# Projections for the next layer in parts of 128 columns, and the denominators of a half in the middle of the next

## The reference

```python
x = x + _L0_xattn_ref(_layernorm(x), ctx_768, Wq, bq, Wk, bk, Wv, bv, Wo, bo)   # 16 heads of 8
...
x = x + _L1_xattn_ref(_layernorm(x), ctx_768, Wq, Wk, Wv, Wo, bo)               # 16 heads of 64
# in _L1_xattn_ref:
k = (context @ Wk).reshape(B, Nk, 16, 64)
v = (context @ Wv).reshape(B, Nk, 16, 64)
```

## Time and profile before

| | |
|---|---|
| three runs, median (lowest, highest) | 3643.95 us (3641.63, 3647.71) |
| profiled execution, span | 3638.8 us |
| first half of layer 0's attention | from 62.14 us to about 161.96 us |
| second half | 161.96 to 260.66 us |
| third half | 260.66 to 359.19 us |
| last half ends | about 852 us |

### The profile page before, as it was taken

How to read it: one execution, slowest core, us unless ns; L and a number is a source line. 1 busy time by engine, 2 the same in 40 slices (tenths; PEclk the granted TensorE clock), 3 DMA queues, 4 the chain that set the end, 5 groups by cost and what they waited for, 6 DMA issues and landing times.

```text
span 3638.8 us, 73817 instructions
## 1 busy us (share of the span) xinstructions
PE 3543.7 (97%) x27546; PEld 1564.5 (43%) x27549; DVE 1858.4 (51%) x1946; ACT 2584.6 (71%) x2742; POOL 857.8 (24%) x1977
## 2 busy tenths in 40 slices
PE   7999999999999999999999999999999999999999
PEld 4333333335544444444444444443222222355654
DVE  4222222224287878797888888763321211155445
ACT  6999999995455555555555555549999999944442
POOL 1222222222222323222322222103332223210000
PEclk9999999999999999999999999999999999999999
DMA  6224232211201111111111111000000000020000
GB/s 201 95 80 111 81 102 83 101 67 53 77 30 40 41 40 41 41 40 41 36 44 36 42 39 41 17 23 6 4 4 4 4 6 27 2 71 14 1 1 6
DMA packets 102892, 163.15 MB, mean 45 GB/s; under 512 B 22452, under 2 KB 43344, under 8 KB 101040
## 3 DMA queue, kind: packets, MB, share of 16 engines
q1 hardware_dynamic: 102576, 158.69, 13.5%
HBM read 93.50 MB, written 65.14 MB: 44 GB/s over the span
## 4 chain that ended last, share of the span: by engine, by line
PE 77%; ACT 13%; issue 6%; DVE 2%; ACTq 1%; DMA 0%; SPq 0%; POOL 0%; DVEq 0%; POOLq 0%
PE ps L1109 20%; PE ps L1083 17%; PE ps L748 11%; ACT probs L1532 8%; ACT probs L1543 5%; PE ps L680 4%; PE ps L570 3%; PE ps L576 3%; PE ps L967 3%; PE ps L1298 2%; PE ps L949 2%; PE ps L1408 1%; PE ps L1425 1%; PE ps L1402 1%; PE ps L1281 1%
## 5 line engine op out<-in xcount | busy, mean ns | idle before, releaser
L1694 ACT ACTIVATE probs<-ps 128x1024 f32<-128x1024 f32 x808 | 783.7, 1023 | 577.1 <-PE ps L1083 309.4
L1543 ACT ACTIVATE probs<-ps 128x1024 f32<-128x1024 f32 x1200 | 1119.7, 1030 | 48.1 <-PE ps L680 41.0
L2715 DVE TENSOR_TENSOR vbuf<-vbuf,probs 128x1024 f32<-128x1024 f32 x784 | 1003.3, 1322 | 204.9 <-ACT probs L1694 201.4
L748 PE MATMUL ps<-probs,vst 128*32 128x512 f32 x6400 | 843.8, 598 | 27.1 <-ACT probs L1543 24.4
L1109 PE MATMUL ps<-probs,klo 128*64 128x512 f32 x1888 | 431.0, 599 | 0.0
L2458 DVE COPY qs<-ps 128x512 f32<-128x512 f32 (+1 forms) x208 | 142.2, 684 | 562.9 <-PE ps L576 279.7
L1932 POOL CAST kst<-kb 128x128 fp32r<-128x128 f32 (+1 forms) x800 | 252.8, 316 | 740.4 <-PE ps L748 593.6
L1532 ACT ACTIVATE probs<-ps 128x1536 f32<-128x1536 f32 x268 | 362.1, 1622 | 3.4 <-PE ps L728 1.8
L1109 PE MATMUL ps<-probs,qs 128*64 128x512 f32 x1376 | 313.7, 599 | 0.0
L1944 POOL COPY vst<-vbuf 128x36 f32<-128x36 f32 (+1 forms) x816 | 193.7, 237 | 438.6 <-PE ps L748 432.1
L2049 POOL CAST keys_b<-keys_a 128x512 fp32r<-128x512 f32 (+1 forms) x90 | 108.7, 1207 | 791.1 <-DMA klo<-kv_scratch 529.1
(11 more groups left out here) (505 smaller groups left out, 4044.9 us busy)
## 6 DMA issues: line engine op xcount, KB each, us to landing
kv_scratch<-qs SPq DMA_DIRECT2D x192, 256.0 KB, 2.0
keys_a<-kv_scratch SPq DMA_DIRECT2D x96, 256.0 KB, 2.6
klo<-kv_scratch SPq DMA_DIRECT2D x56, 256.0 KB, 2.9
qs<-kv_scratch SPq DMA_DIRECT2D x40, 256.0 KB, 2.9
kb<-k_scratch SPq DMA_DIRECT2D x12, 816.0 KB, 6.8
vbuf<-in_L_ffn_W SPq DMA_DIRECT2D x16, 256.0 KB, 3.0
kb<-in_L_ffn_W SPq DMA_DIRECT2D x16, 256.0 KB, 3.0
qz<-q_scratch SPq DMA_DIRECT2D x56, 64.0 KB, 2.1
```

The source lines that it names most:

```text
L748: mm = pe.matmul(ps[band, 6 + half, :], vst[:, r, band], probs[:, r, j * HT:(j + 1) * HT], start=start, stop=stop)
L1543: act.activation(probs[:, r, b * T:(b + 1) * T].rearrange("p (h n) -> p h n", h=2), ps[:, 2 * buf:2 * buf + 2, :], ACT.Exp, scale=HD8 ** - ...
L1694: act.activation(pr1[:, u % BUF1], ps[:, 2 * b:2 * b + 2, :], ACT.Exp, scale=HD64 ** -0.5)\
L2715: dve.tensor_tensor(sum1[:, odd, h], sum1[:, odd, h], e, ALU.add).then_inc(s["added"], 1)
```

## The change

Parts are now 128 columns wide (`GRAIN`), 51 of keys and 51 of values a half. `parts_by_tile` spreads them in proportion to their columns: in the first half over tiles 3 to 50, in the seven others over tiles 1 to 50. In those seven `previous_sums` counts as 512 columns and stands between the last part of keys and the first of values. The wait of a half's first part for `den_copied` becomes one for `acc_copied`; the first part of values now waits for `den_copied`; `previous_sums` also waits for the copy of the last chunk of keys. On DVE `previous8` stands behind the 13 copies of keys.

```diff
-PARTS = 2 * JOBS
-PART_AT = [RING, RING] + [2 * RING + k * (ST - 2 * RING) // (PARTS - 2) for k in range(PARTS - 2)]
+GRAIN = P
+PARTS = [(m, c, p0, min(p0 + GRAIN, CHUNKS[c][1])) for m in range(2) for c in range(NC) for p0 in range(0, CHUNKS[c][1], GRAIN)]
+
+
+def parts_by_tile(first, sums):
+
+    at = [[] for _ in range(ST)]
+    total = sum(p1 - p0 for _, _, p0, p1 in PARTS) + sums * HT
+    begun = 0
+    for m, c, p0, p1 in PARTS:
+        if sums and (m, c, p0) == (1, 0, 0):
+            at[first + begun * (ST - first) // total].append(None)
+            begun += HT
+        at[first + begun * (ST - first) // total].append((m, c, p0, p1))
+        begun += p1 - p0
+    return at
+
+
+PARTS_AT = [parts_by_tile(RING, 0)] + [parts_by_tile(1, 1)] * (2 * NG - 1)
...
                             if half or g:
-                                pe.wait_ge(s["den_copied"], g * 2 + half + DENS[0])
+                                pe.wait_ge(s["acc_copied"], g * 2 + half + SUMS[0] + 2)
+                        if m == 1 and c == 0 and p0 == 0 and (half or g):
+                            pe.wait_ge(s["den_copied"], g * 2 + half + DENS[0])
...
                     pe.wait_ge(s["acc_copied"], gh + SUMS[layer] + 2)
+                    if n == 0:
+                        pe.wait_ge(s["kv_moved"], gh * JOBS + NC + 1)
...
-                            projections1(g, half, [divmod(k // 2, NC) + (k % 2 * (HT // 2), (k % 2 + 1) * (HT // 2))
-                                                   for k in range(PARTS) if PART_AT[k] == t])
+                            for part in PARTS_AT[gh][t]:
+                                if part:
+                                    projections1(g, half, [part])
+                                else:
+                                    previous_sums(gh)
                             av(g, half, at, t % RING, t == 0, t + 1 == ST)
-                            if t == RING - 1 and gh:
-                                previous_sums(gh)
...
-                    previous8(gi, par, half)
                     for m in range(2):
                         if m:
+                            previous8(gi, par, half)
                             dve.reduce_sum(csum[0:C, bass.ds(p, 1)],
```

More of the change, by code:

```diff
@@ L775, in group @@
                         first = (g * 2 + half) * ST + TILES[layer]
-                        stream(first, lambda *at: qk(half, *at), lambda *at: av(g, half, *at), last_sums)
                         if n == 0:
-                            projections1(g, half, [(m, c, 0, HT) for m in range(2) for c in range(NC)])
+                            stream(first, lambda *at: qk(half, *at), lambda *at: av(g, half, *at))
+                            projections1(g, half, [(0, c, 0, HT) for c in range(NC)])
+                            if half or g:
+                                pe.wait_ge(s["kv_moved"], (g * 2 + half) * JOBS + NC + 1)
+                            last_sums()
+                            projections1(g, half, [(1, c, 0, HT) for c in range(NC)])
                         else:
+                            stream(first, lambda *at: qk(half, *at), lambda *at: av(g, half, *at), last_sums)
                             for c in CHUNKS_IN.get(g * 2 + half, ()):
```

## The result

| | before | after |
|---|---|---|
| runs, median (lowest, highest) | 3643.95 us (3641.63, 3647.71) | 3775.59 us (3774.67, 3778.92) |
| span of the profiled execution | 3638.8 us | 3776.6 us |
| ratio after / before, 95% interval | | 1.0364, 1.0352 to 1.0377 |

The kernel is 131.6 us slower by the medians; 138 were forecast, and the time lies in the range of 3745 to 3815 us.

What follows compares the result with a forecast made beforehand. PE was taken to set the pace of layer 0's attention. Boundaries +146, even spread -11, denominators +2 and slots +1 gave +138 us on 3644, so 3782 us, range 3745 to 3815.

Steps and rivals of the forecast that it cites:

- The bound: Layer 0's attention: PE sets the pace, busy 96.69 of 98.53 us in a half; ACT would need 94.2 at most.
- The boundaries of chunks: Two chunks meet in a tile 16 times a half, PE waits for DVE's copy: 1.14 us each, 146 us, bounds 118 and 172.
- The even spread: Parts fill PE's idle time in a half's first tiles: 1.51 us in seven halves, 0.5 in the first, 11.1 won.
- The denominators: Moved to tile 25, DVE's work behind them delays values up to 0.4 us in seven halves: 0 to 3, taken as 2.
- SP and the slots: Third half, fourth chunk's copy waits for a slot that SP's late store frees: some 1.3 us once, 0 to 3.
- Covered copies: Rival: boundary copies fall into PE's slack against ACT, only the even spread's 11 us remain: 3633 us, chance 0.04.
- Narrow matmuls at the price of wide ones: Rival: 128-column matmuls of keys take the 0.46 us of 256, 94 us more in all: 3876 us, chance 0.03.
- The clock: Rival: idle time at the 16 boundaries brings PE's granted clock down, at most 770 us in all, chance 0.02.

Runs made afterwards that it cites:

- twice: The changed kernel with DVE copying each chunk a second time before it gives the bank back: 3874.65 us.
- best2: best with DVE's work behind the denominators cut up, product and context sum moved behind the first and second copies of values: 3631.52 us, ratio 0.9965 to the kernel before.
- cover: The changed kernel with the next chunk's first part written behind the tile's values (`av`) wherever two chunks meet in a tile: 3670.05 us.
- aligned: The changed kernel with a table in which no tile holds parts of two chunks, denominators alone in tile 25: 3653.67 us, ratio 1.0024 to the kernel before.
- narrow: The kernel before, parts in their old tiles, with the matmuls of keys 128 columns wide instead of 256: 3644.17 us.
- best: aligned with SP's loads spread as in loads, and the fifth half's projections over tiles 3 to 50 only: 3643.16 us, ratio 0.9996 to the kernel before.
- loads: The changed kernel with SP's 19 loads for later layers issued one behind each store in the second half, instead of all at its end: 3774.44 us.
- wide: The changed kernel with parts of 256 columns instead of 128, same rule for the tiles: 3664.22 us.
- sums: The kernel before with only the denominators moved behind the last part of keys, their DVE work between copies of keys and values: 3665.69 us.

## Why the prediction was right

**The bound.** PE sets the pace of the attention: each microsecond that it stood, the half grew. twice shows it from one side, best2 from the other: PE's idle time removed came off the half in full.

**The boundaries of chunks**, forecast 146 us with bounds of 118 and 172. Their number was exact. Their price was 1.14 us by the forecast; a steady half grew by 114.37 - 98.54 = 15.83 us, and if the 1.5 us won and the 0.4 lost behind the denominators are taken as forecast, that leaves 16.9 / 16 = 1.06 each, 135 us in all. The timeline gives the same price by itself: parts whose starts stand 1.24 and 1.33 us apart, where 0.23 are the part's own, lose 1.01 and 1.10. The two steps behind it that were a little large are the lag of the copy, 0.58 by one row where it is 0.49 in some boundaries, and the way from copy to PE, 0.10 where it was 0.06. That it is this wait and not the shape of the groups is shown by four runs: cover takes 105 us away without changing a matmul, aligned 122, twice adds what a second copy takes, and narrow changes the matmuls and nearly nothing happens.

**The even spread**, forecast at 11 us won, 1.51 in each of seven halves: the changed kernel has 0.14 us of idle time a half outside the boundaries where 1.84 were, so 1.7 were won there. best shows that hardly anything of it remains (0.3 us a half) once the boundaries are covered, because the start of the half was also the cover for DVE's chain. In best2, with the chain cut, a half is 1.96 us shorter than before. PE's idle time accounts for 1.63 of these; where the rest comes from was not looked into.

**The denominators**, forecast 2 us late, bounds 0 and 3: the wait behind them is 1.2 to 1.3 us against 0.9 elsewhere, 0.3 to 0.4 in each of seven halves, as worked out.

**SP and the slots**, forecast 1.3 us with bounds 0 and 3: this term was mis-sized. The third half grew by 5.0 us more than its neighbours. The copy came due when the forecast said; what was wrong was the 22.2 us taken over for the slot, which came free at 23.7, because SP's queue ran later and longer than before. So 3.0 us went into PE's wait, and 2.0 came from the clock that fell behind it, which was not in the term. The loads run took all 5 away. **The fifth half's** 1.6 us, DVE's loop turning over, was in no term.

**The rivals.** Covered copies: out, by PE's waits. Narrow matmuls at the price of wide ones: out, by narrow, 0.1 us a half. The Trainium skill, page "TensorE: Matmul & The Clock Gate", section "Back-to-back issue gap", has a 128-column matmul far dearer per column than a 512-column one; here, with four matmuls side by side in 32 columns of the array each, the same columns took the same time at 128 and at 256, and a group of 512 columns takes 0.97 us where one of 128 takes 0.24. The measurement decides. The clock: it did not fall at the boundaries, with idle times of 0.8 to 0.9 us, and the fourth half ran as forecast. It did fall in the third half, during and behind 3.91 us of idle time. The Trainium skill, page "TensorE: Matmul & The Clock Gate", section "What's actually happening", has the throttled state as the default and activity as what releases it; the trace agrees as far as it goes, since the clock came back to 1.00 while PE was busy again. At 770 us the rival was the wrong size, at 2 us in one half it was real.

That the sum came within 6.4 us of 131.6 is partly luck. The mechanism and the count were right, but a boundary price 8% too large (11 us) stood against some 5 us in the third and fifth halves that were not foreseen.

## What to carry to other kernels

Before work is spread evenly over an engine that sets the pace, look at what stands between the last use and the next use of each single buffer: here 1.4 us of other matmuls hid 1.0 us of waiting for another engine's copy, and a rule that counted only columns put the two uses side by side 128 times. If the unit of spreading (271 columns a tile) doesn't divide the unit of the buffer (512), align the table to the buffer. And idle time at the start of a stage may be the cover of another engine's chain; move the work there only together with that chain.

## What the runs showed of the hardware

- **Clock after idle time.** In the attention, from its second half on, PE's granted clock fell to the level of 1.2 GHz around every idle time of 3.27 us or more (five, up to 6.15 us, in twice, the changed kernel, cover, wide and aligned). Of seven between 2.27 and 2.76 us it fell around four (2.27, 2.42, 2.62, 2.76) and stayed at 1.00 around three (2.46, 2.58, 2.71); the 2.27 and the 2.58 stand in the same place of the program. Of fifteen between 1.78 and 1.92 us two were followed by a fall (one in twice, one in sums), and none of the shorter ones was. So the length of an idle time alone does not say whether it is paid twice. The slow matmuls lasted a few microseconds and made 3.0 us of waiting into 5.0.
- **A loop's turn on DVE.** At the second turn of a long loop DVE stood 5.25 to 5.6 us (seven runs; 5.55 in the changed kernel, lowest in loads, highest in twice) with no wait that the profile shows. What it does in that time was not looked into.
- **Narrow groups in a row.** Eight matmuls of 128 columns take the 0.46 us of four of 256. One group of four takes 0.24 in front of `av` and 0.35 in front of `qk`. Why the latter is longer stays open.
